# A four-layer graph network on one Trainium2 core: the second edge list stored in dealt order and gathered later, the first layer's one-hots made by ScalarE

## The reference

```python
# edges: src, dst (dst comes sorted), 16 attributes, one of 8 types
x += (segment_sum(h[src], dst) / max(count(dst), 1)) @ W_l.T + b_l + h @ W_r.T        # layer 0, mean
x += concat(h, segsum(w0[type]*h[src], dst), segsum(w1[type]*h[src], dst)) @ W + ...   # layer 1, relations
# layer 2, attention of 4 heads: the edges are grouped by src, keys and values come from dst
k_j = k[dst] + edge_attr @ We ;  alpha = (q[src] * k_j).sum(-1) / sqrt(32)
ex = exp(alpha - m[src]) ;  out = segment_sum(v[dst] * ex / denom[src], src) ; gated with x @ Wskip
x += segment_sum(h[dst], src)                                                          # layer 3, sum
```

## Time and profile before

| | us |
|---|---|
| median of the three timed runs | 12145.74 (12131.86 to 12184.83) |
| span of the profiled execution, first to last instruction | 10339.8 |
| POOL busy | 7070.6 (68% of the span) |
| DVE busy | 6562.4 (63%) |
| PE busy | 6181.9 (60%) |
| ACT busy | 2732.1 (26%) |

### The profile page before, as it was taken

One profiled execution on the slowest core, in us unless ns is written; L12 is line 12 of the kernel. 1 busy time (PEld: TensorE's weight loads), 2 busy tenths in 40 slices (PEclk: granted clock), 3 DMA queues, 4 the chain that ended last, 5 costly groups with the idle time before them and its releaser, 6 DMA issues. The chain is left out here.

```text
span 10339.8 us, 113558 instructions
## 1 busy us (share of the span) xinstructions
PE 6181.9 (60%) x29757; PEld 4616.2 (45%) x29757; DVE 6562.4 (63%) x14941; ACT 2732.1 (26%) x8897; POOL 7070.6 (68%) x7382
## 2 busy tenths in 40 slices
PE   8844577777777746565655656666666434444443
PEld 2223355555555544444444445555555333333333
DVE  7799877777777746666666656666666733333333
ACT  0033211111111114444444425555555400000000
POOL 0056677777777737777777667777777577777776
PEclk6555688888898867777777789999999855555555
DMA  2000132322323233333333334444444422222224
GB/s 89 0 22 11 34 74 72 74 72 72 74 72 74 70 46 56 55 55 55 55 55 55 45 89 112 112 111 111 112 111 111 79 56 54 54 54 54 54 54 59
DMA packets 1357093, 691.02 MB, mean 67 GB/s; under 512 B 1166772, under 2 KB 1207448, under 8 KB 1355688
## 3 DMA queue, kind: packets, MB, share of 16 engines
q0 software_dynamic: 267936, 604.23, 22.4%
q1 hardware_dynamic: 1088520, 79.52, 7.9%
HBM read 579.32 MB, written 103.90 MB: 66 GB/s over the span
## 5 line engine op out<-in xcount | busy, mean ns | idle before, releaser
L1621 POOL DMA_INDIRECT l_kv<-kv_tab,l_words x1616 | 1575.9, 975 | 504.7 <-issue 467.0
L865 POOL DMA_INDIRECT l_rows<-h_tab,l_index x1616 | 1539.1, 952 | 506.6 <-issue 444.4
L1217 POOL DMA_INDIRECT l_rows<-h_tab,l_index x1616 | 1531.5, 948 | 507.5 <-issue 458.4
L557 POOL DMA_INDIRECT l_rows<-h_tab,l_words x1616 | 1524.7, 943 | 515.9 <-issue 411.4
L600 PE MATMUL l_sums<-l_onehot,l_rows 128*128 128x128 f32 x3232 | 826.6, 438 | 1294.9 <-issue 1112.8
L1352 PE MATMUL l_sums<-l_weighted,l_rows 128*128 128x256 f32 x3232 | 1172.6, 527 | 661.9 <-issue 568.0
L600 PEld LDWEIGHTS l_sums<-l_onehot,l_rows 128*128 128x128 f32 x3232 | 719.6, 328 | 1401.9 <-issue 1295.4
L588 DVE TENSOR_TENSOR acc<-acc,l_sums 128x128 f32 x1616 | 464.4, 287 | 1324.1 <-PE l_sums L600 1118.9
L1231 ACT ACTIVATE l_weighted<-l_onehot,l_weights 128x128 f32<-128x128 bf16 x3232 | 987.6, 388 | 1057.8 <-DVE l_onehot L508 1024.5
L1352 PEld LDWEIGHTS l_sums<-l_weighted,l_rows 128*128 128x128 f32 x3232 | 810.4, 263 | 828.9 <-issue 595.0
L1279 DVE TENSOR_TENSOR acc<-acc,l_sums 128x256 f32 x1616 | 678.8, 420 | 676.9 <-PE l_sums L1352 524.5
(11 more groups left out here) (318 smaller groups left out, 10935.4 us busy)
## 6 DMA issues: line engine op xcount, KB each, us to landing
l_rows<-h_tab,l_index POOLq DMA_INDIRECT x3232, 2.5
l_kv<-kv_tab,l_words POOLq DMA_INDIRECT x1616
l_rows<-h_tab,l_words POOLq DMA_INDIRECT x1616, 2.5
l_words<-dealt_src SPq DMA_DIRECT2D x404, 38.0 KB
dealt_src<-h SPq DMA_DIRECT2D x4, 3136.0 KB, 25.3
l_attr<-in_edge_attr SPq DMA_DIRECT2D x44, 272.0 KB, 4.5
h_tab<-h SPq DMA_DIRECT2D x21, 448.0 KB, 3.0
kv_tab<-acc SPq DMA_DIRECT2D x7, 896.0 KB, 4.0
```

Source lines behind the costliest of these rows:

```text
L557: pool.indirect_dma_start(rows[b][:, j, :], None, table, bass.IndirectOffsetOnAxis(ap=words[k % 3][:, at + j, 0:1], axis=0)).then_inc(rows ...
L865: pool.indirect_dma_start(rows[b][:, j, 0:D], None, table, bass.IndirectOffsetOnAxis(ap=index[q // Q16 % WORDS][:, q % Q16 * H + j, :], ax ...
L1217: pool.indirect_dma_start(rows[b][:, j, :], None, h_tab, bass.IndirectOffsetOnAxis(ap=index[q // Q16 % WORDS][:, q % Q16 * H + j, :], axis ...
L1621: pool.indirect_dma_start(kv[s][:, e, :], None, kv_tab, bass.IndirectOffsetOnAxis(ap=words[s][:, e, 0:1], axis=0)).then_inc(kv_ready[b], 16)
```

## The change

1. The second list is not scattered any more. Each deal's 128 chunks go as they are to the DRAM table `staged`, deal after deal, with a plain DMA on SP. For each chunk of the list by_src its row in `staged` is found beforehand: DVE makes the tables ends, rises and owner in rank_phase's second turn (find_chunks); in deal_phase PE looks up, per tile, the ends and rises of its block, ACT copies the rises and DVE counts, in one fused operation per chunk number with a running sum (104 of them, CHUNKS), into chunk_row. In mean_phase POOL gathers 128 chunks at a time by chunk_row (104 indirect DMAs, room for six) and SP stores them in by_src, between its stores of h. The frame of the second list loses beyond, begun and closed, and the deal loses the two small matmuls with shift and ACT's operation for the rows.
2. The one-hots of layer 0's sums are made by ACT (four Abs, one Relu) as 1 - |place - edge's place| cut at 0; DVE only copies the places (where), once per 16 tiles.
3. SP's loads of words are issued up to three buffers ahead, between the stores; `zero` is half as wide and only one row block of `staged` is zeroed; POOL clears the semaphores of the phase before in mean_phase.

```diff
-LISTS = K * TRASH
+CT = P // K                 # 8 chunks to a tile
+SPANS = -(-TILES // P)      # 13
+CHUNKS = SPANS * CT         # 104
+NOWHERE = DEALS * P
@@ rank_phase, SP
-                for at in range(0, ZS, NB * D):
-                    n = min(NB * D, ZS - at)
-                    sp.dma_start(src_flat[:, at:at + n], zero[:, 0:n]).then_inc(zeroed, 16)
+                sp.dma_start(staged[NOWHERE:, :], zero[:, 0:ZS]).then_inc(zeroed, 16)
@@ rank_phase, DVE
+                def in_parts(of, parts):
+                    ch.link(nc.vector.tensor_scalar(high[:], of[:], 6, 6, ALU.logical_shift_right, ALU.logical_shift_left))
+                    ch.link(nc.vector.tensor_copy(parts[0][:], high[:]))
+                    ch.link(nc.vector.tensor_scalar(high[:], of[:], LOW - 1, None, ALU.bitwise_and))
+                    ch.link(nc.vector.tensor_copy(parts[1][:], high[:]))
+                def find_chunks():
+                    nc.vector.scalar_tensor_tensor(line[:, 0:DEALS], stages[:, 0:DEALS], tcol[:, 2:3], back[:], ALU.subtract, ALU.add)
+                    ch.link(nc.vector.memset(line[:, DEALS:], float(NOWHERE + LIFT)))
+                    nc.vector.tensor_copy(rise[:, 0:1], line[:, 0:1])
+                    ch.link(nc.vector.tensor_tensor(rise[:, 1:], line[:, 1:], line[:, 0:DEALS], ALU.subtract))
+                    in_parts(rise, rises)
+                    ch.link(nc.vector.tensor_scalar(line[:], whole[:], tcol[:, 2:3], None, ALU.add))
+                    nc.vector.tensor_copy(rise[:, 0:DEALS], line[:, 0:DEALS])
+                    ch.link(nc.vector.tensor_tensor(rise[:, DEALS:], line[:, DEALS:], tcol[:, 3:4], ALU.add))
+                    in_parts(rise, ends)
+                    ch.link(nc.vector.tensor_scalar(beyond[:], tcol[:, 1:2], tcol[:, 0:1], rest[:, 0:1], ALU.add, ALU.add))
+                    ch.link(nc.vector.scalar_tensor_tensor(owner[:], tile_no[:], beyond[:, 0:1], reached[:], ALU.is_lt, ALU.mult))
...
+                    if turn:
+                        find_chunks()
+                    else:
+                        ch.link(nc.vector.scalar_tensor_tensor(away[0][:], lists[:, 0:DEALS], tcol[:, 2:3], back[:], ALU.add, ALU.subtract))
...
@@ Dealer
+    def store(self, sp, g):
+        r = g % RING
+        sp.wait_ge(self.copied, g + 1)
+        sp.dma_start(self.table[g * P:(g + 1) * P, :], self.out[r].bitcast(I32).rearrange("p k w -> p (k w)")).then_inc(self.sent[r], 16)
@@ Chunks, in deal_phase
+    def vector(self, dve, k):
+        m = k // CT
+        n = span_tiles(m)
+        if k % CT == 0:
+            dve.wait_ge(self.taken, m + 1)
+        if k:
+            dve.wait_ge(self.counted, k)
+        self.nc.vector.scalar_tensor_tensor(self.passed[0:n, :], self.ends_of[m % 2][0:n, 0:DEALS + 1], self.chunk_no[0:n, k:k + 1],
+                                            self.risen[m % 2][0:n, :], ALU.is_le, ALU.mult,
+                                            accum_out=self.total[0:n, k:k + 1]).then_inc(self.counted, 1)
@@ deal_phase, DVE
                     deal.spread_out(dve, k, [(0, WD, words[:, k * GB * GC:min((k + 1) * GB * GC, EC), :])])
+                    if k >= 2:
+                        chunks.vector(dve, k - 2)
+                for k in range(BLOCKS - 2, CHUNKS):
+                    chunks.vector(dve, k)
+                chunks.vector_end(dve)
@@ deal_phase, PE (ACT the same)
+                    if g % (GB * CT) == GB - 1:
+                        chunks.tensor(pe, g // (GB * CT))
@@ sum_deal_phase, SP
+                    if q % Q16 == 2 and WORDS <= q // Q16 + WORDS - 1 < TILES // T16:
+                        load(q // Q16 + WORDS - 1)
                     if q % ATTR == 8 and q // ATTR + 1 < DEALS // ATTR:
                         attributes(q // ATTR + 1)
+                    if q < DEALS:
+                        deal.store(sp, q)
@@ sum_deal_phase, POOL
-                    if LAG <= q < DEALS + LAG:
-                        deal.gpsimd(pool, q - LAG)
-                deal.gpsimd_end(pool)
@@ sum_deal_phase, ACT
+                def one_hots(q):
+                    at = q % Q16 * H
+                    if at == 0:
+                        act.wait_ge(indexed, q // Q16 + 1)
+                    for j in range(H):
+                        last = nc.scalar.activation(apart[q % 2][:, j, :], place[:], ACT.Abs, bias=where[q // Q16 % WORDS][:, at + j, :], scale=-1.0)
+                    last.then_inc(apart_ready, 1)
+                    if q >= RING:
+                        act.wait_ge(summed, pairs_of(q - RING))
+                    act.wait_ge(apart_ready, q + 1)
+                    nc.scalar.activation(onehot[q % RING][:], apart[q % 2][:], ACT.Relu, bias=one[:, 0:1], scale=-1.0).then_inc(oh_ready, 1)
+                for q in range(AHEAD):
+                    one_hots(q)
+                for q in range(QUADS):
+                    if q < DEALS:
+                        deal.scalar(act, q)
+                    if q + AHEAD < QUADS:
+                        if q >= 1:
+                            act.wait_ge(oh_ready, q + AHEAD - 1)
+                        one_hots(q + AHEAD)
@@ sum_deal_phase, DVE
-                    if q + AHEAD < QUADS:
-                        one_hots(q + AHEAD)
@@ mean_phase
+            def _(sp):
+                for k in range(CHUNKS):
+                    sp.wait_ge(fetch_ready[k % FETCH], 16 * (k // FETCH + 1))
+                    m, n = k // CT, span_tiles(k // CT)
+                    sp.dma_start(lists[k % CT, m * P:m * P + n], fetched[k % FETCH][0:n]).then_inc(fetch_stored[k % FETCH], 16)
+                    r = k // SHARE - 1      # SHARE = 15
+                    if k % SHARE == SHARE - 1 and r >= 0:
+                        sp.wait_ge(h_ready, r + 1)
+                        sp.dma_start(rows[r], h[:, part_of(r), :]).then_inc(h_stored, 16)
...
+            def _(pool):
+                for k in range(CHUNKS):
+                    if k >= FETCH:      # FETCH = 6
+                        pool.wait_ge(fetch_stored[k % FETCH], 16 * (k // FETCH))
+                    n = span_tiles(k // CT)
+                    pool.indirect_dma_start(fetched[k % FETCH][0:n], None, staged, bass.IndirectOffsetOnAxis(ap=chunk_row[0:n, k:k + 1], axis=0)
+                                            ).then_inc(fetch_ready[k % FETCH], 16)
+                for sem in done_with:
+                    pool.sem_clear(sem)
```

More of the change, by code:

```diff
@@ L163, in ranks_of @@
             return (sb(f"chunk_{name}", [P, EC], F32, where), sb(f"slot_{name}", [P, EC], F32, where),
-                    sb(f"first_{name}", [BINS, DEALS + 1], F32, where), sb(f"open_{name}", [BINS, DEALS], F32, where),
-                    [sb(f"shift_{part}_{name}", [BINS, DEALS], BF16, where) for part in ("high", "low")])
+                    sb(f"first_{name}", [BINS, DEALS + 1], F32, where), sb(f"open_{name}", [BINS, DEALS], F32, where))
         x = sb("x", [P, NB, D])
@@ L257, in rank_phase @@
         lists = sb("lists", [BINS, DEALS + 1])
+        stages = sb("stages", [BINS, DEALS + 1])
+        rest = sb("rest", [BINS, 1])
+        beyond = sb("beyond", [BINS, 1])
+        line, rise = sb("line", [BINS, DEALS + 1]), sb("rise", [BINS, DEALS + 1], I32)
+        high = sb("high", [BINS, DEALS + 1], I32)
         reached = sb("reached", [BINS, TILES], BF16)
@@ L642, in __init__ @@
         frame = lambda name: sb(name, [BINS, GB, P], BF16)
-        self.begun, self.beyond = frame("begun"), frame("beyond")
-        self.closed, self.left, self.next = ([frame(f"{name}{b}") for b in range(2)] for name in ("closed", "left", "next"))
-        self.rows = sb("rows", [P, RING], I32)
+        self.left, self.next = ([frame(f"{name}{b}") for b in range(2)] for name in ("left", "next"))
         ps = lambda name: own.enter_context(nc.psum_tensor(f"{tag}_{name}", [P, 512], F32))
@@ L716, in tensor @@
             pe.wait_ge(self.copied, g - 1)
-        for part in range(2):
-            nc.tensor.matmul(self.sums[b][:, size:size + 1], self.closed[k][:, i, :], self.shift[part][:, g:g + 1],
-                             start=(part == 0), stop=(part == 1))
+        self.tensor_rows(pe, g)
         if at == 0:
@@ L764, in deal_phase @@
+def deal_phase(nc, ranks, shift, words, place, trash, table, sent, done_with, ends, rises, owner, chunk_no, chunk_row):
     with ExitStack() as own:
-        deal = Dealer(nc, own, "dst", ranks, WD, BF16, GB, place, trash, table, sent)
+        deal = Scatterer(nc, own, "dst", ranks, shift, WD, BF16, GB, place, trash, table, sent)
+        chunks = Chunks(nc, own, ends, rises, owner, chunk_no, chunk_row)
+        BLOCKS = -(-DEALS // GB)
         with nc.Block() as block:
@@ L772, in _ @@
                     deal.gpsimd(pool, g)
-                deal.gpsimd_end(pool)
+                deal.all_sent(pool)
             @block.scalar
@@ L811, in sum_deal_phase @@
         index = [sb(f"index{b}", [P, T16, 1], I32) for b in range(WORDS)]
```

(4 more changed lines are left out.)

226 lines of the change are left out of this document (160 added, 66 removed).

## The result

Measured: 11703.5 us (median of four runs, 11658.2 to 11705.8) against 12149.5 for the kernel before, ratio 0.9622 with an interval of 0.960 to 0.9644. The forecast was 11736, range 11690 to 11890, so it is 33 us off and inside its range. The step from before to after is -446 us, forecast was -410.

What follows compares the result with a forecast made beforehand. POOL, by its number of DMA instructions, was taken to bound the sum stage, DVE the first dealing stage. +6 + 53 - 514 + 45 = -410 us from 12145.7 gave 11736 us, range 11690 to 11890.

Steps and rivals of the forecast that it cites:

- What bounds the sum stage: First layer's sums: POOL's number of DMA instructions sets the stage; without 391 scatters 2023 us against 2536.5, -514 us.
- Is the rest fast enough?: First layer's sums: PE, ACT and DVE stay under POOL's 5.0 us a quad, at 3.7 (high clock), 3.3 and 3.3.
- Sort stage: Second turn of the sort: find_chunks stands in DVE's uncovered chain, net +6 us (4 to 8).
- Chunk count: Stage dealing the first list: fused DVE operations, 0.55 us each on the path, 96 in the loop, +53 us.
- Mean stage: Mean stage: 104 gathers at POOL's pace of 1.29 us, room for six, 142 us against 97, +45 us.
- Rival A: Mean stage held by its ring of six or the DMA engines: +87 in place of +45, 11778 us; chance 0.2.
- B: Sum stage misses POOL's pace, PE at low clock half the time: -354 in place of -514, 11896 us; chance 0.12.
- C: Sum stage: gaps keep PE's clock low throughout, PE bounds at 7.1 us a quad, slower, 12556 us; chance 0.04.
- D: Sum stage: POOL waits for sums or rows each quad, 5.8 us a quad, 12056 us; chance 0.02.
- E: First list's dealing: chunk count takes 1.1 us on the path, +106 in place of +53, 11789 us; chance 0.03.
- the 1806 us between them lie around the span: Whole kernel: the difference between profiled span 10339.8 us and timed median 12145.74 lies outside the span and stays unchanged.
- Rival F: Whole kernel: what lies around the span shrinks with it, -481 us, 11665 us; chance 0.05.

## Why the prediction was right

- **What bounds the sum stage** (POOL, by its number of transfers; -514): right, -520, of which 506 are the scatters (504 forecast) and 14 shorter gathers. Leaving the scatters out alone gives 476 of it, putting a fifth transfer back costs 489. Taking another gather stage as the model (2023) was within 7 us.
- **Is the rest fast enough?** PE 3.7 us a quad and a clock of 0.9 or above: 3.9 and 0.97. ACT 3.3, of them 0.4 of waits: busy 2.5. DVE 3.3: 3.4. "Moving the one-hots to ACT is worth 0 by itself": 4 us. What the sentence does not say is that without any relief of DVE POOL's pace is missed by 42 us: in the changed kernel part 2 is worth nothing because part 1 has already relieved the stage.
- **Sort stage** +6: +4.6. **Chunk count** +53: +52. It took 0.61 us, with a separate row of 0.07 for the read of the sum; in the timeline the next block starts 7.06 us after the last (forecast 7.05), so the neighbours' overlap was rightly taken off. Rows of DVE in the changed kernel, to set beside the earlier trace rows:

```profile
745.00 0.68 DVE L827 TENSOR_TENSOR dst_beyond<-dst_table,open_dst 64x512 bf16<-64x512 f32 x1
...
751.52 0.61 DVE L903 SCALAR_TENSOR_TENSOR chunks_passed<-chunks_ends_of,chunk_no,chunks_risen 128x392 f32<-128x392 f32 x1
752.06 0.07 DVE L903 DVE_READ_ACCUMULATOR chunks_passed<-chunks_ends_of,chunk_no,chunks_risen 128x1 f32 x1
752.06 0.68 DVE L827 TENSOR_TENSOR dst_beyond<-dst_table,open_dst 64x512 bf16<-64x512 f32 x1
```

- **The halving for two non-bf16 SBUF inputs** of the Trainium skill (Vector Engine (DVE) Microarchitecture Reference, Points that are easy to get wrong): not seen. The moved count has both inputs in SBUF, in f32, and takes 0.60 to 0.62 us for 392 columns, as it does with one in PSUM.
- **Mean stage** +45: +51. The 104 gathers start 1.36 us apart, not 1.29, and the ring is at its limit. The round of 7.2 us (measured: 7.5) was nearly right by luck: it added the gather's 0.99 and the store's 0.36 to landings that already hold them, and it took landings of 2.5 and 2.9 us that were 4.0 and 3.2 with six in flight. Rival A (+87) did not come.
- **Rivals B, C, D** (a slow PE, a POOL that waits) did not come: clock 0.97, POOL waits for PE 41 us. **E** neither: 0.5 us on the path a chunk, not 1.1.
- **The step that was wrong is the first one**: "the 1806 us between them lie around the span". In the changed kernel's timed runs such time lies inside the span, as stops; for the kernel before it is the likely reading, since without stops only 1.7 us lie around its span. Taking them as unchanged was nearly right by luck: they are 12149.5 - 10339.3 = 1810 us before and 11703.5 - 9925.8 = 1778 after. So of the 446 us measured, 413 are the change and 33 are a difference in what the stops cost. The check "2015 to 2080 us in the sum stage" failed in the profile that came with the result (2424.5 us, with a clock of 0.85 and 192 us of waits for PE, where 0.9 or more and under 100 were said) and held without stops (2016.5, 0.97, 41). Rival F (the rest shrinks in proportion) was nearer to the truth in sign than the forecast, and wrong in size.

## What to carry to other kernels

Where an engine issues indirect transfers back to back, count them: 1.25 to 1.29 us each here, and a transfer that another queue can issue plainly costs that engine nothing (the stores on SP; the gathers that they made necessary cost 51 us in the mean stage). Before taking work off a second engine, ask whether the first still holds the stage: the one-hots were worth at most 4 us or 42, by what else DVE had to do. Move helper work (here the count) from the stage in which its engine is the bound to one in which another engine is; the 52 us it costs can be had back almost whole. Before a difference between a profile's span and the timed runs is set aside as lying around the span, compare the spans of the timed runs.

## What the runs showed of the hardware

**Stops.** In the first measurement's profile of the changed kernel, several engines sit idle at the same time for some 2 to 7 us, some 100 times in each gather stage. In the last sum stage, timeline of all engines:

```profile
9501.47 2.05 PE L646 MATMUL l_sums<-l_onehot,l_rows 128*128 128x128 f32 x8 [3.57 <-DMA l_rows<-h_tab,l_words]
9502.31 0.72 DVE L634 TENSOR_TENSOR acc<-acc,l_sums 128x128 f32 x2 [2.77 <-remote]
...
9503.83 0.95 POOL L603 DMA_INDIRECT l_rows<-h_tab,l_words  x1 [0.30 <-issue]
9507.20 0.71 DVE L634 TENSOR_TENSOR acc<-acc,l_sums 128x128 f32 x2 [4.18 <-remote]
9507.20 0.36 SPq L590 DMA_DIRECT2D l_words<-by_src  x1
9507.81 0.94 POOL L603 DMA_INDIRECT l_rows<-h_tab,l_words  x1 [3.02 <-remote]
```

DVE, SP and POOL resume within 0.6 us of each other, and in the code each waits for sums that PE reports. They don't stop together: POOL still issues a gather at 9503.83, 0.8 us after DVE's last operation ended. This fits a PE whose sums come late at least as well as a core that stands still; which of them it is was not settled. PE's ends are modelled, so the row of 2.05 us does not contradict a PE that stopped halfway. Against the execution without stops the stages lose 408 us (sums), 335 (relations), 632 (attention) and 297 (last sum), and the dealing stage, at the same low clock as the last sum, 1 us. First and last gather of attention and of the last sum in it:

```profile
L1840 POOL DMA_INDIRECT l_kv<-kv_tab,l_words x1616: 940/946/6695, 6507.5 to 9216.1; - x180
...
L603 POOL DMA_INDIRECT l_rows<-h_tab,l_words x1616: 938/944/965, 9313.6 to 11626.6; - x180
```

What stops the engines stays open: no profiled run of the experiments had these stops, so nothing could be tried on them.

**Gathers that all read one row land late.** In the version without scatters the empty list sends every row of a gather to row 0 of its table. The last sum's gathers, landing in 2.5 us (median) in the changed kernel, then take 15.8, and attention's 9.1 in place of 2.8; each stage grows by some 700 us. With the 43 us of the sum stage the two are what that version has over its expected 9820 us:

```profile
L557 POOL DMA_INDIRECT l_rows<-h_tab,l_words x1616: 938/944/962, 8520.4 to 11264.8; - x180
...
  PE l_sums L600: 761.8, 360
...
DMA to landing us min/median/max: 3.5/15.8/22.8
```

That it is the one row, and not the one place in a block to which all sums then go, was not separated.
